# Emptying a slot table piece by piece ahead of its ids, and moving three DRAM copies behind the s stores, in a recurrent and routed kernel

## The reference

```python
x = L0_attn_inputs                       # (4, 2048, 512), 8192 tokens
xn = _layernorm(x)                       # over the last axis
# h = h * A + xn_t along the sequence, then s = h @ BC       (512 x 512)
s = _L0_attn_ref(xn, L0_attn_A, L0_attn_BC)
# each token picks one of 8 experts: argmax over xn @ gate_w.T
# z = xn + xn @ expert_w[chosen]                             (512 x 512 each)
g = _silu(_L0_ffn_ref(xn, L0_ffn_gate_w, L0_ffn_expert_w))
return x + s * g
```

## Time and profile before

| | |
|---|---|
| median of 3 runs | 524.4 us (523.9 to 524.87) |
| profiled execution, its own time | 521.92 us |
| its span | 520.2 us |
| mean granted TensorE clock | 0.987 |
| PE busy | 495.5 us (95% of the span) |
| DVE, ACT, POOL busy | 409.0, 260.2, 325.1 us |
| DMA | 116.99 MB, mean 225 GB/s |

### The profile page before, as it was taken

How to read it: one execution, slowest core, us unless ns; L and a number is a source line. 1 busy time by engine, 2 the same in 40 slices (tenths; PEclk the granted TensorE clock), 3 DMA queues, 4 the chain that set the end, 5 groups by cost and what they waited for, 6 DMA issues and landing times. The chain is left out here.

```text
span 520.2 us, 10723 instructions
## 1 busy us (share of the span) xinstructions
PE 495.5 (95%) x2739; PEld 389.0 (75%) x2740; DVE 409.0 (79%) x1075; ACT 260.2 (50%) x500; POOL 325.1 (62%) x362
## 2 busy tenths in 40 slices
PE   7959999999999999999996999999999999999993
PEld 6647777777777777777675788888888888887882
DVE  5968998999999998899752777777778777776773
ACT  4647678667767766776621333333333333333330
POOL 3446766676676667667765466666676666656652
PEclk9979999999999999999999999999999999999997
DMA  8996878787788878777336676777767776766620
GB/s 243 394 342 178 258 241 247 233 269 227 253 258 234 249 237 263 228 243 234 120 97 193 224 226 222 234 239 244 249 213 234 235 243 214 232 221 212 222 82 9
DMA packets 65538, 116.99 MB, mean 225 GB/s; under 512 B 8906, under 2 KB 26378, under 8 KB 65428
## 3 DMA queue, kind: packets, MB, share of 16 engines
q1 hardware_dynamic: 47328, 64.59, 39.3%
q0 software_dynamic: 18176, 52.06, 31.6%
HBM read 66.30 MB, written 57.48 MB: 238 GB/s over the span
## 5 line engine op out<-in xcount | busy, mean ns | idle before, releaser
L1073 PE MATMUL ps_s<-w_hi,split 128*128 x284 | 118.2, 416 | 0.2
L643 ACT ACTIVATE ps_s<-ps_s 128x512 f32<-128x512 f32 x71 | 41.3, 582 | 151.4 <-PE ps_s L1075 151.4
L509 POOL DMA_INDIRECT out_dram<-work x71 | 73.7, 1038 | 65.9 <-DVE work L890 52.3
L1074 PE MATMUL ps_s<-w_lo,split 128*128 x284 | 112.4, 396 | 0.0
L1075 PE MATMUL ps_s<-w_hi,split 128*128 x284 | 112.3, 395 | 0.0
L418 POOL TENSOR_TENSOR split<-work,split 128x1024 fp32r<-128x1024 f32 x32 | 77.0, 2406 | 48.4 <-ACT split L571 48.4
L977 PE MATMUL ps_s<-bc_hi,split 128*128 128x512 f32 x256 | 104.6, 409 | 0.5 <-ACT split L571 0.5
L978 PE MATMUL ps_s<-bc_lo,split 128*128 128x512 f32 x256 | 101.5, 396 | 0.0
L436 POOL DMA_INDIRECT slot_table<-token_id,slot_id x64 | 63.0, 985 | 35.2 <-issue 17.3
L499 POOL DMA_INDIRECT work<-token_rows,work x67 | 70.9, 1058 | 21.5 <-issue 19.8
L872 DVE TENSOR_SCALAR work<-work 128x512 f32<-128x512 f32 x71 | 39.3, 554 | 46.1 <-DMA work<-token_rows,work 35.7
(11 more groups left out here) (118 smaller groups left out, 740.1 us busy)
## 6 DMA issues: line engine op xcount, KB each, us to landing
token_rows<-work SPq DMA_DIRECT2D x31, 528.0 KB, 3.2
work<-in_L_attn_inputs_dram SPq DMA_DIRECT2D x31, 512.0 KB, 4.7
token_rows<-work SPq DMA_DIRECT2D x29, 512.0 KB, 5.5
work<-in_L_ffn_expert_w_dram SPq DMA_DIRECT2D x128, 64.0 KB, 3.8
slot_table<-w_lo SPq DMA_DIRECT2D x1, 4160.0 KB, 17.7
token_rows<-in_L_attn_inputs_dram SPq DMA_DIRECT2D x3, 512.0 KB, 13.8
out_dram<-work POOLq DMA_INDIRECT x71, 3.4
work<-token_rows,work POOLq DMA_INDIRECT x67, 4.5
```

Source lines behind the costliest of these rows:

```text
L509: nc.gpsimd.indirect_dma_start(out=out_flat, out_offset=bass.IndirectOffsetOnAxis(ap=slot_tok[:, n:n + 1], axis=0), in_=o_sb[:, u], in_off ...
L1073: nc.tensor.matmul(z_ps[v], hi, wh, start=(k == 0), stop=False)
L1074: nc.tensor.matmul(z_ps[v], hi, wl, start=False, stop=False)
```

## The change

The table is no longer filled by one transfer. SP empties it in 32 pieces, one for each group: piece g covers, in each of the 8 experts' lists, the 256 slots in which the first token of that rank can come with group g, 8 x 16 KB, in runs of 512 bytes. The eight rows at the table's end are a transfer of their own. Pieces 0 and 1 stand ahead of the loop; piece c+2 stands in round c, behind `load_w` and ahead of `store_s`. POOL's scatter of group c waits for piece c. The source is now a tile of its own (`empty_ids`, 128 numbers wide), so DVE's wait ahead of the last four groups is gone. The first four rounds are written out ahead of the loop, and the three copies of x stand behind the s stores of rounds 0, 1 and 2.

```diff
-    FILL = 640
+    FILL = 128
+    NEW = GT // P
...
-    table_fill = table.rearrange("r q -> (r q)").rearrange("(p n f) -> p n f", p=P, f=FILL)
+    table_g = table[0:E * TOKENS // P].rearrange("(e g u) q -> g e (u q)", e=E, u=NEW).rearrange(
+        "g e (s f) -> g s e f", f=FILL)
+    table_end = table[E * TOKENS // P:].rearrange("r (s f) -> (r s) f", f=FILL)
...
-        empty_ids = w_lo[:, BLOCKS - 2:, :].rearrange("p b d -> p (b d)")[:, 0:FILL].bitcast(I32)
...
+        empty_ids = sb("empty_ids", [P, FILL], I32)
...
+            def empty(it, c):
+                wait(sp, table_empty[c % 2], 16 * rounds(4, it, c, 2))
+                nc.sync.dma_start(table_g[4 * it + c], empty_ids[0:NEW * P * LINE // FILL].unsqueeze(1).to_broadcast(
+                    [NEW * P * LINE // FILL, E, FILL])).then_inc(table_empty[c % 2], 16)
...
             sp.wait_ge(empty_ready, 1)
-            nc.sync.dma_start(table_fill, empty_ids.unsqueeze(1).to_broadcast([P, TROWS * LINE // FILL, FILL])).then_inc(table_empty, 16)
-            for c in range(XR - 1):
-                copy_x(0, c)
+            for c in range(2):
+                empty(0, c)
+            nc.sync.dma_start(table_end, empty_ids[0:8 * P * LINE // FILL]).then_inc(end_empty, 16)
             sp.wait_ge(pad_ready, 1)
-            with sp.Fori(0, GROUPS // 4 - 1) as it:
+
+            def round_of(it, c):
+                next_x(it, c)
+                store_x(it, c + XR - 1)
+                load_w(it, c + WR)
+                empty(it, c + 2)
+                store_s(it, c)
+
+            for c in range(4):
+                round_of(0, c)
+                if c < XR - 1:
+                    copy_x(0, c)
+            with sp.Fori(1, GROUPS // 4 - 1) as it:
                 for c in range(4):
-                    next_x(it, c)
-                    store_x(it, c + XR - 1)
-                    load_w(it, c + WR)
-                    store_s(it, c)
+                    round_of(it, c)
...
+                if c + 2 < GROUPS:
+                    empty(0, c + 2)
...
-                pool.wait_ge(table_empty, 16)
+                pool.wait_ge(table_empty[c % 2], 16 * (rounds(4, it, c, 2) + 1))
...
+                pool.wait_ge(end_empty, 16)
...
-                if c == GROUPS - 4:
-                    dve.wait_ge(table_empty, 16)
```

More of the change, by code:

```diff
@@ L220, in bass_recurrent_routed @@
         w_loaded = [sem(f"w_loaded{v}") for v in range(WR)]
-        table_empty = sem("table_empty")
+        table_empty = [sem(f"table_empty{v}") for v in range(2)]
+        end_empty = sem("end_empty")
         id_stored = [sem(f"id_stored{v}") for v in range(2)]
@@ L366, in _ @@
         def _(pool):
-            nc.gpsimd.memset(empty_ids, EMPTY).then_inc(empty_ready, 1)
+            nc.gpsimd.memset(empty_ids[:, :], EMPTY).then_inc(empty_ready, 1)
             nc.gpsimd.memset(ident[:, :], 0.0).then_inc(const_ready, 1)
```

## The result

The changed kernel takes 519.74 us in the median of 4 runs (519.63 to 520.45); the kernel before took 524.15 us beside it (523.9 to 524.87, 4 runs). The ratio is 0.9916, with a 95% interval of 0.9899 to 0.9934: 4.4 us faster, where 5.6 were forecast. The profiled execution took 519.75 us, on the median of its kernel; the one of before had been 2.2 us under the median of its own, so the two spans, 520.2 and 518.0 us, show less of a gain than the runs do. Most of that lies in stage 2: from POOL's first gather (266.67 us before, 261.41 us after) to the end of the span it is 253.5 us before and 256.6 us after, where the second profile of the changed kernel has 253.5 us; a stretch of half clock at 283.5 to 287 us (mean 0.51) can account for up to 1.7 us of it.

A forecast was written before the change was run, and what follows sets the result against it. PE sets the steady group's 7.58 us; early in stage 1 late x transfers stall it. 4.32 + 1.73 - 0.45 - 0 = 5.6 us off 524.4 gives 518.8 us; forecast range 517.4 to 520.3 us (chance 0.69).

The forecast's parts named there:

- the stall: Stage 1, 29.75 to 35.37 us: PE waits 5.25 us behind ACT's 4.32 us wait for the x store; gain 4.32 us.
- its tail: PE's next group, partly at low clock, lasts 9.31 us against 7.58; that 1.73 us goes too, bounds 0 and 1.73.
- the copies' term: Copies of x behind the s stores of rounds 0 to 2 make ACT late: cost 0.45 us, bounds 0 and 1.35.
- The pieces: One piece per round for thirty groups, behind the weight loads: 0.35 to 1.1 us of engine time, hidden; cost 0 us.
- The rival of the held queue: Pieces' small packets overfill the DMA engines' idle time in about 28 rounds: slower, 527.2 us; chance 0.09.
- The 2.0 us: Fixed part of a DMA: 33 transfers for one, estimated 64 us more latency, changing nothing as nobody waits for them.
- POOL's wait for the fill: POOL's 2.85 us wait goes as well; counted at nothing, as group 2's low part waits for ACT until 29.94 us.
- one round's worth: Of three rounds with a copy, each up to 0.45 us late, only one was counted: 0.45 us.
- The price of a copy in the queue: A 512 KB copy's time on the DMA engines in rounds 0 to 2: 1.5 us, from 1.1 to 1.9.

The follow-up runs named there:

- e4: Changed kernel (pieces kept) with the three copies of x moved to the head of rounds 28, 29 and 30: 517.27 us, ratio 0.9883 to the kernel before.
- e5: Kernel before, its one 4.26 MB fill kept, with the three copies moved to rounds 28 to 30: 517.79 us, ratio 0.9894 to the kernel before.
- e3: Kernel before, its one 4.26 MB fill kept, with only the three copies moved behind the s stores: 519.64 us, ratio 0.9933 to the kernel before.
- e8: Changed kernel with the copies of rounds 0 to 2 between the weight loads and the piece: 519.33 us, ratio 0.9868 to the kernel before.
- e1: The changed kernel run again unaltered, with a second profile: 517.68 us, ratio 0.9899 to the kernel before.

## Why the prediction was right, and where it was not

The time lies in the range, and the mechanism is the one forecast for the stall and its tail; the copies' term was too small. One reading of the page was loose: it shows a single early dip of the clock, in the third slice, and no other in the first ones.

**The stall.** Predicted: ACT's and DVE's waits go, PE keeps 0.93 of its 5.25 us. Measured: no wait of either, PE keeps 0.84 us, and group 1 is 4.39 us shorter, against 4.32. That this rest is ACT's own chain and not the DMA agrees with every variant: 0.82 to 0.85 us in all of them, wherever fill and copies stand. The x load of group 4 was issued at 16.96 us, 0.9 us before the forecast's 17.9, as POOL's memset that SP waits for ended at 16.93 us instead of 17.77 us, like the whole program start.

**The tail.** Predicted: 1.73 us, gone with the clock's dip. The clock is at 1.00 in groups 2 to 4, so it is gone; e2 and e4 show group 2 at 7.63 us once nothing else holds it, against 9.31: 1.68 us.

**The pieces.** Predicted at 0 with 0.35 to 1.1 us of engine time each: measured 0.62 us each, hidden. Over twenty groups before and after:

```profile
82.58:234.78 152.20, 152.13 (x941) 115.54 (x940) 138.87 (x480) 110.61 (x221) 104.07 (x121) 1.00 0.80 246
```

```profile
77.53:229.45 151.92, 151.92 (x942) 115.43 (x940) 138.37 (x480) 110.68 (x221) 103.88 (x121) 1.00 0.88 264
```

7.61 and 7.60 us a group, at a DMA share of 0.80 and 0.88: the forecast said 0.81 to 0.9. The rival of the held queue is dead: the 32 transfers of 128 KB land in 3.3 us in the median, and no engine waits for one. The Trainium skill, DMA: Bandwidth & Descriptors, section Rules for kernel authors, says to coalesce many small transfers into one large one, since under 64 KB one pays mostly overhead. The pieces lie above that size, and not coalescing them cost no time here. The 2.0 us that the prediction took from the section on the anatomy of a DMA, on that page of the Trainium skill, are given there for transfers issued by POOL; SP issues the pieces, and no run shows a fixed part.

POOL's wait for the fill was put at nothing too. In the kernel before nothing of it shows beside the stall; e5 puts it at up to 0.85 us of group time once the stall is gone, by way of POOL's low part and DVE, a path that the prediction did not have.

**The copies: the term that was mis-sized.** The prediction took 0.45 us, "one round's worth", with 1.35 us as its upper bound. They cost 1.84 us (8.21 + 8.55 + 7.82 less three times 7.58), 2.1 us in the second profile; against e2 it is 1.7 and 2.0 us, over the upper bound too. The price of a copy in the queue was right for two of three rounds: an x store behind one was forecast to land in 5.5 + 1.5 = 7.0 us, and the three landed in:

```profile
DMA to landing us min/median/max: 7.1/7.3/7.9
```

The second, issued at 37.86 us, took the 7.9 us (45.77 - 37.86), 0.9 us over the forecast.

The step that failed is the count and size of the late rounds: "I take one round's worth, 0.45 us". One round was struck out with "In the first of them the spare is larger (44.68 - 41.84 = 2.84 us between the same two rows)". Those 2.84 us were read in the group of the tail, in which PE ran at the low clock for part of the time; it was PE that was late there, not ACT early. At full clock the distance is 37.22 to 38.35 us, 1.13 us where ACT is late, and 1.21 us in e2's same group (37.59 to 38.80 us), where it is not: only 0.1 us of spare, so ACT's 0.54 us of wait reached PE nearly whole and the round lasts 0.62 us more. The second round was later still (0.95 us of wait), as its x store landed late. So each of the two took more than the 0.45 us allowed for one. The third x store came just in time (45.92 + 7.3 = 53.2 us, ACT's row at 53.29 us), and that round is 0.23 us long for a reason that no wait of ACT names in this profile; in the second one ACT waits 0.16 us there. With 0.62 + 0.96 + 0.23 in the sum it would have read 4.32 + 1.73 - 1.81 = 4.24 us, where the groups moved by 4.28 us; as both are read from the same groups this is no second proof. The medians cannot judge a term of this size: they moved by 4.4 us in one set and 5.4 us in the other.

**What made the stall.** The prediction put the lateness of the two transfers on the fill and the copies together and did not ask what either would do alone. e2 and e3 answer: taking away either the fill's bulk or the copies ends the wait in group 1. The 4.26 MB are in by about 28 us with the copies behind them or without (POOL goes on at 28.10 us before, 27.47 us in e5), and the first x store is wanted at 29.94 us. So the pieces, the larger part of the edit, are needed for 0.9 us if the copies go elsewhere, and for the whole 6 us if these stay where they were. Of the changed kernel's two halves, the second one undoes nearly a third of what the first one gives (1.7 to 2.0 of 6.0 us).

**The better version.** e2, the pieces with the copies left ahead of the loop, has the lowest median measured: 515.49 us against 517.68 us of the changed kernel on the same chip. Its interval (0.9824 to 0.9879) lies under the changed kernel's median ratio of 0.9899, with a small overlap of the two intervals; the shorter groups 2 to 4 are what speaks for it beyond the medians.

## What to carry to other kernels

When two bulk transfers ahead of a loop delay its first loads, remove one of them before moving both: the other may then drain before the first transfer behind it is wanted, as it did here. When a bulk transfer is moved behind another one in the loop, compare the landing of the *next* transfers in the same queue with the time at which each is wanted, round by round. And read that time from a group at full clock: a distance between two engines that is taken in a group where one of them ran slowly is no spare.

## What was not expected of the hardware

The packets of a small write cost almost nothing each: 1024 packets of 128 bytes in place of 256 of 512 bytes added 0.2 us to the 0.62 us of a 131 KB piece.

Group 0 of nearly the same program starts at different times. The first score transposes stand at 13.04 us in the first profile of the changed kernel, 14.10 in its second, 13.87 and 14.37 in the two of before, 16.05 in e8. POOL's first memset shrank from 640 to 128 numbers a row (0.63 to 0.20 us), which lets PE start 0.43 us sooner (3.83 to 3.40 us), but the spread is larger than that, and I count none of it as the change's. In stage 2's head the second profile of the changed kernel has a mean granted clock of 0.89 in a stretch where e2's has 1.00:

```profile
270.00:285.00 15.00, 11.81 (x51) 9.21 (x52) 5.78 (x11) 3.30 (x6) 6.04 (x6) 0.89 0.70 213
```

```profile
270.00:285.00 15.00, 12.38 (x59) 9.05 (x58) 7.30 (x14) 3.48 (x7) 5.50 (x7) 1.00 0.61 196
```

The two kernels are alike there, up to 2 us of shift. Over the twelve profiles stage 2, from POOL's first gather on, lasts 252.9 to 256.6 us, though no edit touches it; a dip near its head is in five of them. Such dips and the spread of the start may be part of why single runs of one kernel differ by over 4 us (516.13 to 520.82 in e1); only one run of each set has a profile, so this is not shown. It is why a difference of 2 us was read from the groups first and from the medians second.
